# The first block of the feed-forward part prepared inside the last attention step's level chain

## What is computed

```python
sa, ca, ga, sb, cb, gb = silu(c) @ wmod                      # per sequence
h = layernorm(x) * (1 + ca) + sa
x = x + ga * attn(h)          # gated delta rule, 16 key heads x 2 value heads, state 128 x 128 each
h = layernorm(x) * (1 + cb) + sb
x = x + gb * (keep_2_of_4(silu(h @ w_gate) * (h @ w_up)) @ w_down)
```

## Time and profile before

| what | us |
|---|---|
| median of 3 runs (lowest, highest) | 2014.25 (2011.45, 2016.29) |
| the profiled execution, whole | 2010.74 |
| its span, first to last instruction | 2009.0 |
| PE, DVE, ACT, POOL busy in the span | 1947.9, 1800.0, 1737.5, 1382.2 |
| mean granted clock of PE | 0.988 |
| PE busy in 1825 to 1870 us (45 us), clock | 32.86, 0.77 |
| PE and DVE busy in 1867 to 2009 us (142 us) | 135.75, 130.07 |

### The profile page before, as it was taken

The page is one execution under the profiler, slowest core; times in us unless marked ns, Lnnn a source line. Parts: engine busy times, 40 slices in busy tenths (PEclk is TensorE's granted clock), DMA queues, the critical chain, the costliest instruction groups (busy, mean ns, idle before and its releaser), DMA issues.

```text
span 2009.0 us, 63635 instructions
## 1 busy us (share of the span) xinstructions
PE 1947.9 (97%) x24518; PEld 1656.9 (82%) x24518; DVE 1800.0 (90%) x2901; ACT 1737.5 (86%) x3588; POOL 1382.2 (69%) x962
## 2 busy tenths in 40 slices
PE   6699999999999999999999999999999999997999
PEld 5478888888888888888888888888888888886787
DVE  6889999999999999999999999999999999985997
ACT  4699999999999999999999999999999999986332
POOL 6367777777777777777777777777777777764452
PEclk9799999999999999999999999999999999998899
DMA  3000000000000000000000000000000000003000
GB/s 117 13 23 3 3 24 3 24 2 24 3 24 3 24 2 4 22 3 23 3 24 3 24 3 24 3 24 2 3 24 3 24 3 2 24 3 115 6 27 22
DMA packets 17596, 35.75 MB, mean 18 GB/s; under 512 B 5772, under 2 KB 14092, under 8 KB 14996
## 3 DMA queue, kind: packets, MB, share of 16 engines
q1 hardware_dynamic: 17300, 31.68, 4.7%
HBM read 29.04 MB, written 2.64 MB: 16 GB/s over the span
## 4 chain that ended last, share of the span: by engine, by line
PE 91%; DVE 3%; POOL 2%; issue 2%; ACT 1%; DMA 0%; POOLq 0%; SPq 0%; DVEq 0%; ACTq 0%
PE bank L647 81%; PE bank L650 10%; DVE tt L1677 0%; ACT yl L1282 0%; DVE b_le L1667 0%; POOL a_lo L520 0%; DMA o<-in_x 0%; POOL go L541 0%; POOL invT L557 0%; POOL y_acc L564 0%; POOL osq L513 0%; DVE ae L1831 0%; DVE oss L1899 0%; POOL f_small L572 0%; POOL e_b L505 0%
## 5 line engine op out<-in xcount | busy, mean ns | idle before, releaser
L1796 DVE SCALAR_TENSOR_TENSOR cc<-bank,wc,cc 128x510 f32<-128x510 f32 (+2 forms) x768 | 558.7, 740 | 13.4 <-ACT cc L1307 3.7
L647 PE MATMUL bank<-h,w 128*128 128x512 f16 (+1 forms) x1920 | 422.4, 361 | 5.6 <-DVE cc L1796 5.5
L647 PEld LDWEIGHTS bank<-h,w 128*128 128x128 f16 x1920 | 173.9, 98 | 140.9 <-DVE cc L1796 6.6
L486 POOL TENSOR_TENSOR rn<-n2m,mhalf 128x4 f32<-128x4 f32 x64 | 64.8, 1012 | 280.8 <-DVE n2m L1812 280.8
L1392 ACT ACTIVATE inv<-bank 128x512 f16<-128x512 f32 x384 | 244.7, 637 | 11.5 <-PE bank L647 11.5
L1397 ACT ACTIVATE invT<-bank 128x512 f16<-128x512 f32 x384 | 246.5, 642 | 1.3 <-PE bank L647 1.3
L1860 DVE TENSOR_TENSOR yl<-bank,mask 128x512 f16<-128x512 f32 x320 | 218.9, 684 | 6.5 <-PE bank L647 6.4
L647 PE MATMUL bank<-inv,a 128*128 128x64 f16 (+1 forms) x3584 | 217.4, 197 | 4.1 <-ACT inv L1392 3.9
L1307 ACT ACTIVATE cc<-bank,wc 128x512 f32<-128x512 f32 x256 | 177.8, 695 | 33.3 <-PE bank L647 33.2
L647 PEld LDWEIGHTS bank<-inv,a 128*128 128x128 f16 x3584 | 179.7, 98 | 16.5 <-ACT inv L1392 5.2
L647 PE MATMUL bank<-w,goT 128*128 128x256 f16 x1536 | 190.8, 275 | 1.4 <-DVE goT L1912 1.4
(11 more groups left out here) (230 smaller groups left out, 5504.1 us busy)
## 6 DMA issues: line engine op xcount, KB each, us to landing
w_raw<-in_wh SPq DMA_DIRECT2D x15, 1032.0 KB, 5.0
v<-in_x SPq DMA_DIRECT2D x4, 512.0 KB, 4.0
out<-sol SPq DMA_DIRECT2D x16, 128.0 KB, 1.7
moving<-rank_store SPq DMA_DIRECT2D x64, 8.0 KB
standing<-rank_store SPq DMA_DIRECT2D x64, 8.0 KB
w_raw<-in_wgate SPq DMA_DIRECT2D x1, 1024.0 KB, 5.0
cc<-in_wup SPq DMA_DIRECT2D x1, 1024.0 KB, 4.8
pt<-gate_store SPq DMA_DIRECT2D x2, 512.0 KB, 5.1
```

The source lines that it names most:

```text
L486: gp.tensor_tensor(rn[:], n2m[:, blk(s), 0], mhalf[:, 0:TL], ALU.pow).then_inc(sig("rn"), 1)
L647: return mm(o_, l_, r_, start=start, stop=stop, skip_group_check=True)
L1796: V.scalar_tensor_tensor(dst, src, wc[:, par(s), i, 3 - j:4 - j], dst, ALU.mult, ALU.add).then_inc(sig(f"conv{i}"), 1)
```

## The change

No arithmetic is changed. What is done on tiles 0 to 3 moves from the end of body 64 and from body 65 into body 64, and `gate(0)` and `up(0)` move forward in body 65.

The input of block 0 and the two gate rows of block 0 get places of their own, so that they can be loaded during body 63 and 64:

```diff
-x_f = [v[:, i].rearrange("p t v d -> p (t v d)").rearrange("p (t c) -> p t c", c=C) for i in range(2)]
+x_v = [v[:, i].rearrange("p t v d -> p (t v d)").rearrange("p (t c) -> p t c", c=C) for i in range(2)]
+x_f = [flat(e_b[:])[:, 0:1024].rearrange("p (t c) -> p t c", c=C), x_v[0], x_v[1], x_v[0]]
...
+gates_0 = kn[:].rearrange("p r t s -> p (r t s)")[:, 0:BG * C].rearrange("p (g c) -> p g c", c=C)
```

SyncE issues them after the last transposes of the normed keys, and after `at` and `pt` of step 63:

```diff
     def load_inputs(b):
-        sp.dma_start(x_f[b % 2], x_t[b]).then_inc(sig(f"f_x_{b % 2}"), 16)
+        sp.dma_start(x_f[b], x_t[b]).then_inc(sig(f"f_x_{b % 2}"), 16)
...
     def load_gates(dst, kind, half):
...
+    sp.wait_ge(sig("knt_ps"), STEPS)
+    sp.dma_start(gates_0, gate_store[0:BG, 0:C].unsqueeze(0).broadcast_to([P, BG, C])).then_inc(sig("f_g0"), 16)
+    sp.wait_ge(sig("at"), STEPS)
+    sp.wait_ge(sig("pt"), STEPS)
+    load_inputs(0)
...
     sp.wait_ge(sig("u0_ps"), STEPS - 1)
-    load_inputs(0)
+    load_inputs(1)
...
     sp.wait_ge(sig("u0_ps"), STEPS)
-    load_inputs(1)
+    load_inputs(2)
     sp.wait_ge(sig("o1_ps"), STEPS)
-    load_gates(gates_a, 0, 1).then_inc(sig("f_ga"), 16)
+    load_gates(gates_a, 0, 1).then_inc(sig("f_gb"), 16)
...
     for j in range(NT):
-        if j % TL == 0 and j // TL + 2 < NB:
-            need(sp, "x2_ready", j + TL)
-            load_inputs(j // TL + 2)
+        if j == 0:
...
+            sp.wait_ge(sig("x2_ready"), 2 * TL)
+            load_inputs(3)
```

GpSimd: `add_input` 0 to 3 go behind `first_inverse(63)`, ahead of `output_scale(61)`; `hidden_rstd` 0 to 3 and `hidden_low` 0 and 1 close body 64; in body 65 `scaled_low(63)` stands ahead of `output_scale(62)`:

```diff
     def add_input(j):
...
         pool.wait_ge(sig(f"f_x_{j // TL % 2}"), (j // TL // 2 + 1) * 16)
-        gp.tensor_tensor(y_acc[:, j], y_acc[:, j], x_f[j // TL % 2][:, j % TL], ALU.add).then_inc(sig("x2_ready"), 1)
+        gp.tensor_tensor(y_acc[:, j], y_acc[:, j], x_f[j // TL][:, j % TL], ALU.add).then_inc(sig("x2_ready"), 1)
...
     def hidden_rstd(j):
...
             first_inverse(s1)
+            if not s0:
+                for j in range(TL):
+                    add_input(j)
...
-    def last_bodies(s0, s1, s2, s3):
-        gate_output(s3)
-        if s2:
-            for j in range(TL):
-                add_input(j)
-        if not s2:
-            hidden_low(2)
-            hidden_low(3)
-        output_scale(s3)
-        if s2:
-            scaled_low(s2)
-        scaled_output(s3)
-        if s2:
+        if s1 and not s0:
             for j in range(TL):
                 hidden_rstd(j)
             hidden_low(0)
             hidden_low(1)
...
+    def last_bodies(s0, s1, s2, s3):
+        gate_output(s3)
+        if s2:
+            scaled_low(s2)
+        output_scale(s3)
+        scaled_output(s3)
+        if s2:
+            hidden_low(2)
+            hidden_low(3)
```

TensorE: `turn_hidden` 0, 1 go behind the first z product, 2, 3 behind the second; `gate(0)` goes behind `first_values(63)`, `up(0)` behind `second_values(63)`:

```diff
             z_rows(0, s1)
+            if not s0:
+                turn_hidden(0)
+                turn_hidden(1)
...
             z_rows(1, s1)
+            if not s0:
+                turn_hidden(2)
+                turn_hidden(3)
...
     def turn_hidden(j):
         pe.wait_ge(sig("xn"), NT + j + 1)
-        bk = bank[7 - j // 2] if j < TL else bank[1]
+        bk = bank[2 + j // 2] if j < TL else bank[1]
...
-            pe.wait_ge(sig("x_ready"), STEPS * NL)
-            pe.wait_ge(sig("xt_ready"), STEPS * NL)
-            pe.wait_ge(sig("yt"), STEPS)
+            pe.wait_ge(sig("iv"), STEPS)
+            pe.wait_ge(sig("pt"), STEPS)
+            pe.wait_ge(sig("at"), STEPS)
+            pe.wait_ge(sig("vv"), STEPS * 2)
+            pe.wait_ge(sig("kx"), STEPS)
+            pe.wait_ge(sig("kxl"), STEPS)
...
-            pe.wait_ge(sig("iv"), STEPS)
-            pe.wait_ge(sig("pt"), STEPS)
-            pe.wait_ge(sig("vv"), STEPS * 2)
+            pe.wait_ge(sig("f_hT"), TL * CK)
...
     def up(u):
...
             pe.wait_ge(sig("f_w_lo"), 8)
-            pe.wait_ge(sig("f_hT"), TL * CK)
...
+            pe.wait_ge(sig("x_ready"), STEPS * NL)
+            pe.wait_ge(sig("xt_ready"), STEPS * NL)
+            pe.wait_ge(sig("yt"), STEPS)
...
             first_values(s2)
+            gate(0)
...
             first_output(s2)
-            turn_hidden(0)
-            turn_hidden(1)
...
             second_values(s2)
-            turn_hidden(2)
-            turn_hidden(3)
+            up(0)
...
             second_output(s2)
-            gate(0)
...
         project_output(1, s3)
-        if s2:
-            up(0)
```

ScalarE: `hidden_turned` 0, 1 in body 64, 2, 3 around `refined(63)`, the high halves of the up weights later, `gate_silu(0)` from body 66 into body 65:

```diff
             act.wait_ge(sig("n2"), STEPS * 2)
-            act.wait_ge(sig("z_ps"), STEPS * 2)
-        bk = bank[7 - j // 2] if j < TL else bank[1]
+        if j % TL == 0:
...
+            act.wait_ge(sig("z_ps"), (STEPS - NB + b + 1) * 2)
+        bk = bank[2 + j // 2] if j < TL else bank[1]
...
             z_tanh(0, s1)
+            if not s0:
+                hidden_turned(0)
+                hidden_turned(1)
...
     def last_bodies(s0, s1, s2, s3):
-        if not s2:
-            gate_silu(0)
-        if s2:
-            up_weights_high(0, 2)
+        if s2:
+            hidden_turned(2)
             refined(s2)
-            up_weights_high(2, 4)
+            hidden_turned(3)
...
             first_kept(s2)
+            up_weights_high(0, 2)
             first_output(s2)
-            hidden_turned(0)
-            hidden_turned(1)
+            up_weights_high(2, 4)
         output_high(0, s3)
+        if s2:
+            gate_silu(0)
...
             second_kept(s2)
-            hidden_turned(2)
-            hidden_turned(3)
```

VectorE: `gated` 0 to 3 and two low halves of the gate weights behind `level_rows(1)`, the rest of those behind `second_rest(62)`, statistics and normalising between levels 3 to 5; `hidden_product(0)` from body 66 into body 65:

```diff
     def gated(j):
         dve.wait_ge(sig("ya"), (STEPS - NB + j // TL + 1) * 2)
-        dve.wait_ge(sig("f_ga"), (j // 8 + 1) * 16)
-        V.scalar_tensor_tensor(y_acc[:, j], y_acc[:, j], Y_SCALE, gates_a[:, j // CH], ALU.mult,
+        if j < TL:
+            dve.wait_ge(sig("f_g0"), 16)
+        else:
+            dve.wait_ge(sig("f_gb" if j // 8 else "f_ga"), 16)
+        gates_j = gates_0[:, j // CH] if j < TL else gates_a[:, j // CH]
+        V.scalar_tensor_tensor(y_acc[:, j], y_acc[:, j], Y_SCALE, gates_j, ALU.mult,
...
     def hidden_stats(j):
...
             level_rows(1, s1)
+            if not s0:
+                for j in range(TL):
+                    gated(j)
+                gate_weights_low(0)
+                gate_weights_low(1)
...
             second_rest(s2)
+            if not s0:
+                gate_weights_low(2)
+                gate_weights_low(3)
...
             if not s0:
-                gate_weights_low(0)
-                gate_weights_low(1)
+                hidden_stats(0)
+                hidden_stats(1)
...
             second_output(s2)
+            if not s0:
+                hidden_normed(0)
+                hidden_normed(1)
+                hidden_stats(2)
+                hidden_stats(3)
...
             level_rows(4, s1)
+        if s2:
+            output_sums(s2)
             if not s0:
-                gate_weights_low(2)
-                gate_weights_low(3)
-        if s2:
-            output_sums(s2)
+                hidden_normed(2)
+                hidden_normed(3)
...
             z_gate(1, s1)
-            if not s0:
-                for j in range(TL):
-                    gated(j)
...
     def last_bodies(s0, s1, s2, s3):
         if s2:
-            for j in range(TL):
-                hidden_stats(j)
-            for j in range(TL):
-                hidden_normed(j)
...
             up_weights_low(1)
+            second_rest(s2)
...
             hidden_stats(TL)
-            hidden_product(0)
-        if s2:
-            second_rest(s2)
+        output_low(0, s3)
+        if s2:
...
             up_weights_low(3)
-        output_low(0, s3)
...
             gated(TL)
+            hidden_product(0)
```

## The result

| | median us (lowest, highest) | ratio to before, 95% interval |
|---|---|---|
| before, 8 runs beside it | 2011.84 (2009.18, 2016.29) | |
| after, 8 runs | 2019.29 (2017.38, 2021.75) | 1.0038 (1.0029 to 1.0047) |

The change makes the kernel 0.38% slower, about 7.6 us. The profiled execution of after took 2021.75 us with a span of 2020.0, so 11.0 more than that of before. From there to VectorE's last `add_output` it is 66.12 us in before and 75.02 in after: the drain is 8.9 us longer. The loop is not: in the 142 us behind that point PE is busy for 135.76 and DVE for 130.10, against 135.75 and 130.07.

What follows compares the result with a forecast made beforehand. TensorE bounds up to body 64, VectorE the feed-forward loop, and list order the drain between. The drain's delays and gains left VectorE's loop entry +5.5 us late: 2019.8 us against a 2014.25 median, 8-in-10 range 2012.5 to 2024.

Steps and rivals of the forecast that it cites:

- rival (c): Drain heavier: half clock reaches `up(0)`, +2.6, or a table load, +1.3; +7 to +9.5 total; chance 0.15 with late loads.
- GpSimd's queue: Body 64: the four adds stand ahead of `scaled_low(62)` on GpSimd, so `key_state(62)` starts 7.8 us later.
- Half clock and the lists to level 4: Rest of body 64: half clock +1.9, VectorE's list before the level 4 mask +1.75, smaller terms; `refine(63)` +11.1.
- Body 65: From `refine` to `second_output`, 20.9 us becomes 18.25, with `gate(0)` free in idle time; `second_output(63)` +8.5.
- From the up weights to `second_output`: Body 65, ScalarE: behind the up weights at 1850.5, table load 1.28, then three pairs of about 1.1, reaching 1855.1.
- The order of GpSimd's list in body 65: Step 62's scale and `scaled_output` follow `scaled_low(63)`, 1.9 + 1.9 us, so `turn_output(62)` comes at 1847.2.
- Body 66: `turn_output(63)` +7.0, projection start +6.1; projection 4.73 at half clock or about 3.5; VectorE enters the loop +5.5.
- (a): Rival of no hole in body 64, `key_state(62)` not held: total -0.9 to about -3, 2011 to 2013.5; chance 0.10.
- The signs: What would show it: 8 us idle before `key_state(62)`, clock 0.50, `refine(63)` near 1837, `up(0)` near 1850.5, loop near 1873.
- Silu's table: In the drain: Square after Silu adds no table load; if outside Silu's set, one more of 1.28, sum +6.8.

Runs made afterwards that it cites:

- e3: Changed kernel plus 75 products nobody reads, filling TensorE's hole ahead of `key_state(62)` in body 64; ratio to before 1.0034.
- e4: Changed kernel with `hidden_stats` 2 and 3 behind the mask of level 4 on VectorE; ratio to before 1.0032.
- e5: Changed kernel with `up(0)` back behind the last projection of step 62 on TensorE, Silu left in body 65; ratio to before 1.0032.
- e7: Changed kernel with step 62's `output_scale` and `scaled_output` ahead of `scaled_low(63)` on GpSimd in body 65; ratio to before 1.0028.
- e1: Changed kernel with the four `add_input` of body 64 behind `scaled_output(61)` on GpSimd; ratio to before 1.0016.
- e8: Changed kernel with body 64's `add_input` behind `scaled_output(61)` on GpSimd, `gated` 0 to 3 and two weight low halves behind `second_rest(62)` on VectorE; ratio to before 1.0014.
- f1: Kernel before, without the change, bodies 65 and 66 reordered: step 63's chain first on each engine, feed-forward work after it; ratio to before 0.9943.

## Why the prediction came out as it did

The predicted time, 2019.8, lies 0.5 from the median of 2019.29, and that flatters it. I added +5.5 to a base 2.4 above the 2011.84 of the runs beside it, and the shift was +7.6 in the time and +8.9 at the last add. Two errors of 2 to 3 us went against each other. By the size of the shift it is rival (c), but by none of (c)'s mechanisms: half clock did come behind the 2.97 us of idle in body 65, but `up(0)` ran at full clock (its 24 products took 2.8 us), and there was one table load in the drain. Slower was right, by the mechanism that I put first. Step by step, as starts behind `turn_system(63)` less those of before:

| step | predicted | measured |
|---|---|---|
| `key_state(62)` | +7.8 | +8.5 |
| `refine(63)` | +11.1 | +11.6 |
| `second_output(63)` | +8.5 | +10.2 |
| `turn_output(63)` | +7.0 | +8.8 |
| start of the projection | +6.1 | +8.3 |
| last `add_output` | +5.5 | +8.9 |

*GpSimd's queue: right, a little small.* The four adds took 3.25, `gated` to last add 3.75 as worked out. The scale began 7.8 later, as predicted. But I carried the 3.98 from the scale to `us` over from before, and it took 4.75 (1812.69 to 1817.44): beside the two weight halves `osc` took 0.65 and 1.97 instead of 0.20 and 1.64, and VectorE's halves 1.69. I had written that the weights "fall in the hole and cost nothing"; they lay in the hole, but beside the GpSimd work for which the hole waited, and lengthened it.

*Half clock and the lists to level 4: right in sum.* e3 gives 2.0 for a forecast 1.9, and from `key_state(62)` to `refine` it was +3.1 where I had +3.3. The mask of level 4 came 1.73 later behind its product than before, where I had 1.75. But I added this to ScalarE's `hidden_turned`, and e4 shows that the two cover each other: with 1.1 of VectorE's part gone, ScalarE's copy was no earlier.

*Body 65: the term that was mis-sized.* I had 18.25 from `refine` to `second_output`; it was 19.47. `gate(0)` was free, and at full clock. The step that failed is "1.9 + 1.9, so `turn_output(62)` at 1847.2", 46.5 behind `turn_system(63)`; it came at 47.76 (1850.55). From the end of `us` (1845.77) to that of `go` (1850.41) it took 4.64 instead of 3.8: again the pair of `osc`, 0.65 and 1.97, now beside VectorE's up weights. Then `turn_output(62)` itself ran at half clock behind its 2.97 of idle, 1.09 instead of 0.60, which I had not counted either. `refine` was 0.5 later than I had it, too. Everything behind it moved with it: ScalarE's high half, VectorE's last up weights, and with these Silu and `up(0)` (1854.4, 51.6 behind, where I had 49.8).

*From the up weights to `second_output`: the right length by the wrong path.* I had 4.6 us on ScalarE: the table load, then three pairs of copies. It took 4.5, but the table load (1852.38 to 1853.66) was over before the weights came, and ScalarE's high half waited 1.17 us for the second half of `turn_output(62)`, which stood behind the 2.8 us of `up(0)` on TensorE. I had priced `up(0)` as waiting, never as being waited for. That the two lengths agree is luck; e5, which takes `up(0)` out of the way, gains 1.4 here.

*The order of GpSimd's list in body 65.* e7 shows what GpSimd's order was worth here: 2.5 us to `second_output`. I had it in the sum as a wait; that it could be taken away by exchanging two calls I had not seen.

*Body 66: the mechanism right, the clock lower than I took it.* To `turn_output(63)` the gain was 1.4, forecast 1.5. Then transposes and projection ran wholly at half clock, 1.94 and 5.29. I had taken between 3.5 and 4.73 for the projection; this is 1.2 of the 3.4 that were missing at the end, counted from the middle of my two ends. 1.7 more came with `second_output`, 0.1 up to `turn_output(63)`, and 0.4 between it and the projection (2.65 us where I had 2.2). The longer idle time ahead doesn't explain the 5.29: behind the same idle time e1, e4 and e8 took 4.29, 4.09 and 4.12. What sets the moment at which the clock comes back is not shown, so this term was uncertain by more than 1 us however well the rest was known.

*The rival of no hole.* I priced (a) at -0.9 to -3. e1 tried it and came to +3.6 at the last add. The step that failed there is that, with GpSimd's queue free, the chain would go on as before but for the 2.2 of the weights: VectorE's `gated` also stands before mask 2, and I had counted it at nothing because in the change it lies in the hole. Take the cover away, and the masks of levels 1 and 2 are 7.89 us apart (e1) instead of 2.84 (before): 5.05 where I had 2.2. At `refine` (a) comes to +4.7 by my prices and e1 measured +6.7; 1.9 more are body 65, 20.1 us where I had 18.25.

*The signs.* `key_state(62)` with 8.9 us idle (the trace names no releaser, only "issue"), clock 0.50 behind it, the mask of level 4 1.73 later behind its product, `gate(0)` in the idle, `up(0)` behind the last up weights and `turn_output(63)` after more than 5 us of idle came as written; `refine` stood at 1839.43 against the 1836.85 of the sum, 2.1 of the 2.6 being the later start of the drain. The later signs were further off: `up(0)` 3.9, `turn_output(63)` 3.8 and VectorE's entry into the loop 5.5 us behind the stated moments, with the same 2.1 in each.

## What to carry to other kernels

Work that has slack is still not free in a queue that runs in order: put it behind every instruction that the chain waits for, not where the engine first looks idle. Here some 6 us of VectorE work and 3.3 us of GpSimd work, with 2.0 for the half clock behind the hole, cost 11.6 us inside a level chain. With the chain first on every engine, and `gate(0)` and `up(0)` behind the last solution instead of ahead of it, they filled a wait that was idle anyway, and the projection that ended it ran at full clock (f1, 0.57% faster than before; the shares of the single calls were not taken apart). A cover must be priced on every engine that shares it: taking away one wait (e1) showed the next one, which it had hidden.

## What the runs showed of the hardware

*VectorE and GpSimd lengthen each other.* A 128x256 f32 pass of VectorE with both inputs in SBUF, `gated(4)`, took 2.28 us in after, started 0.34 behind a GpSimd operation on 128x1024 of 2.34 (1863.30), and ended 0.28 behind its end; the next one, `gated(5)`, with GpSimd idle, took 0.42 (1878.41). Four of them took 2.48 beside the adds alone and 5.10 in e1. Two 128x512 passes took 1.28 alone, 1.69, 2.34 and 3.64 beside different operations; GpSimd's 128x8 add 0.20 and 0.65, its power 1.64 and 1.97, its `us` 1.15 and 1.60. VectorE's masks, which read PSUM, kept their 0.69, for one at 1806.29 in before, beside GpSimd's low half. The rows show that each is longer beside the other, not by which part of the chip. The Trainium skill, GPSIMD Engine Reference, section "8. Key points", says that GpSimd shares its SBUF interfaces with VectorE and contends with VectorE instructions that have two SBUF inputs or run in a 2-port performance mode. The rows agree with the first: the gating and the weight halves have two, the masks have one. Two inputs are not needed, though: `hidden_normed`, a pass with one 128x256 input in SBUF, took 0.40 with GpSimd idle (1881.10 in after) and 0.89 beside GpSimd's `hidden_low` in e4 (1832.14). Which mode it ran in, no trace here shows. That section gives no price; these rows do.

*Silu's table.* Square of step 63 came after Silu and brought no second load: the only one in the drain is that of 1852.38. By the Trainium skill, ScalarE: Activation LUTs, section "Table sets: the hidden batching unit", cheap functions are in every set; the trace agrees, for Square, which that sentence doesn't name.
